# Routing scatters of a mixture-of-experts stage: order of the last group's powers, and how many scatters are under way

## What is computed

```python
probs = softmax(x @ Wr)                       # x: the normed tokens, N = 32*112
w_topk, e_topk = top_k(probs, 2)
e_flat = e_topk.reshape(-1)
pos = cumsum(one_hot(e_flat)) - 1, taken at e_flat
keep = pos < 1024
buf = zeros(8, 1024, 256).at[e_flat, pos].set(repeat(x, 2), mode='drop')
h = rms(buf, norm_w)
buf_out = (gelu(h @ Wg) * (h @ Wu)) @ Wd + buf
contrib = w_topk * buf_out[e_flat, pos] * keep
out = x + contrib.sum   # tokens that overflowed take a small shared expert instead
```

## Time and profile before

| | |
|---|---|
| median of 3 runs | 3072.48 us |
| lowest and highest | 3069.31 and 3073.73 us |
| span of the profiled execution | 3069.1 us, the only time shown of it |
| busy: PE, DVE, ACT, POOL | 2945.7, 2030.9, 1448.5, 650.4 us |
| DMA | 185.47 MB, mean 60 GB/s |

### The profile page before, as it was taken

One profiled execution on the slowest core, in us unless ns is written; L12 is line 12 of the kernel. 1 busy time (PEld: TensorE's weight loads), 2 busy tenths in 40 slices (PEclk: granted clock), 3 DMA queues, 4 the chain that ended last, 5 costly groups with the idle time before them and its releaser, 6 DMA issues. The chain is left out here.

```text
span 3069.1 us, 61161 instructions
## 1 busy us (share of the span) xinstructions
PE 2945.7 (96%) x23332; PEld 2275.7 (74%) x23332; DVE 2030.9 (66%) x4378; ACT 1448.5 (47%) x2845; POOL 650.4 (21%) x952
## 2 busy tenths in 40 slices
PE   8997999989899999999999999799999999899999
PEld 6874656567799999999999999577777777556444
DVE  5773111138577887788888877566767666589664
ACT  3431111126455555555555555476666666556000
POOL 4565000046100220013012200212212112036000
PEclk9997999999899999999999999899999999899999
DMA  9643233249300000000000000000000000337100
GB/s 292 214 128 106 82 117 110 88 144 299 104 1 2 1 2 1 2 1 1 2 1 2 1 2 1 24 25 22 17 22 22 17 22 17 106 108 227 51 14 21
DMA packets 79537, 185.47 MB, mean 60 GB/s; under 512 B 12981, under 2 KB 23202, under 8 KB 78916
## 3 DMA queue, kind: packets, MB, share of 16 engines
q1 hardware_dynamic: 62708, 141.50, 14.3%
q10 hardware_dynamic: 10208, 25.30, 2.8%
q0 software_dynamic: 6336, 14.76, 1.7%
HBM read 150.26 MB, written 27.79 MB: 58 GB/s over the span
## 5 line engine op out<-in xcount | busy, mean ns | idle before, releaser
L2792 DVE CUSTOM_DVE_ANT_0 probs<-ps,add 112x375 f32<-112x375 f32 x512 | 258.9, 544 | 82.7 <-PE ps L2945 76.0
L2871 ACT ACTIVATE probs<-probs,neg_top 112x375 f32<-112x375 f32 x512 | 278.5, 600 | 63.5 <-DVE neg_top L2792 60.1
L1734 DVE TENSOR_TENSOR hidden<-gated,ps 128x512 f32<-128x512 f32 x64 | 44.0, 687 | 294.7 <-PE ps L1777 294.7
L2972 PEld LDWEIGHTS ps<-ident,probs 112*125 112x125 f32 x1536 | 196.8, 188 | 44.4 <-issue 16.7
L2351 DVE TENSOR_REDUCE top<-ps 112x16 f32<-112x1792 f32 x96 | 194.2, 2023 | 46.1 <-PE ps L2590 45.9
L2972 PE MATMUL ps<-ident,probs 112*125 112x112 f32 x1536 | 219.7, 279 | 1.8 <-DVE probs_t L2799 1.8
L3416 PE MATMUL ps<-we,xn_t 128*128 128x512 f32 x448 | 201.9, 614 | 1.7 <-PEq L846 0.9
L2367 DVE TENSOR_TENSOR probs<-probs,inv_sum 112x1792 f32<-112x1792 f32 x96 | 196.0, 2042 | 3.3
L2355 DVE TENSOR_TENSOR probs<-ps,top 112x1792 f32<-112x1792 f32 x96 | 194.3, 2024 | 3.3
L2363 DVE TENSOR_REDUCE row_sum<-probs 112x16 f32<-112x1792 f32 x96 | 193.9, 2020 | 3.2 <-ACT probs L2475 3.2
L2558 PE MATMUL ps<-ident,probs 112*112 112x112 f32 x1536 | 179.8, 260 | 8.2 <-ACT probs_t L2470 7.3
(11 more groups left out here) (464 smaller groups left out, 6276.8 us busy)
## 6 DMA issues: line engine op xcount, KB each, us to landing
ctx_t<-in_ctx_T_dram SPq DMA_DIRECT2D x96, 375.0 KB, 4.5
ctx_sb<-in_ctx_dram ACTq DMA_DIRECT2D x64, 384.0 KB, 4.5
ctx_sb<-in_ctx_dram SPq DMA_DIRECT2D x32, 384.0 KB, 8.9
ctx_sb<-in_ctx_T_dram SPq DMA_DIRECT2D x32, 375.0 KB, 3.1
queue<-zeros SPq DMA_DIRECT2D x32, 256.0 KB, 5.1
rows<-queue SPq DMA_DIRECT2D x16, 512.0 KB, 4.9
outputs<-out SPq DMA_DIRECT2D x16, 512.0 KB, 2.9
mask_in<-in_mask_BxSxS_fk_dram SPq DMA_DIRECT2D x16, 328.1 KB
```

The lines of the kernel that those rows point to most:

```text
L2792: dve.tensor_tensor_reduce(out=probs[:, u, h, :], in0=k.ps[0:S, SCORE + h, 0:L], in1=add[:, j % 2, :], scale=1.0, scalar=BIG, op0=ALU.add, ...
L2871: act.activation(probs[:, u, h, :], probs[:, u, h, :], ACT.Exp, bias=neg_top[:, u, h:h + 1], scale=-1.0).then_inc(s["probs_done"], 1)
L2972: mm = pe.transpose(k.ps[0:KR, PT + h % 2, r * S:(r + 1) * S], probs[:, n % 3, h, r * KR:(r + 1) * KR], k.ident[0:S, 0:S])
```

## The change

Only POOL's instruction list changes. In `shared_scatters`, `token_sizes` and `token_inverses` of group 3 stand ahead of the 32 scatters. The stop behind every fourth scatter is gone; instead each scatter adds to one of three semaphores in turn (`landed[0..2]`), and before scatter i POOL waits until scatter i - 3 has landed. At the end it waits for all three. Groups 0 and 1 keep their own semaphores and waits. `token_scatter` takes the semaphore as an argument.

```diff
-    t.scattered = [sem(nc, f"scattered{g}") for g in range(B // G)]
+    t.scattered = [sem(nc, f"scattered{g}") for g in range(LAST - 1)]
+    t.landed = [sem(nc, f"landed{i}") for i in range(UNDER_WAY)]
...
+UNDER_WAY = 3
...
 def shared_scatters(k, w, t, pool):
 
     token_half_scales(k, w, pool, GH * (LAST + 1) - 1)
-    for g in (LAST - 1, LAST):
-        for n in range(G * TOP_K):
-            token_scatter(k, t, pool, g, n)
-            if g == LAST - 1 and n == 3:
-                token_sizes(k, w, pool, LAST)
-            elif g == LAST - 1 and n == 7:
-                token_inverses(k, w, pool, LAST)
-            if n % 4 == 3:
-                pool.wait_ge(t.scattered[g], 16 * (n + 1))
-    for g in range(LAST + 1):
+    token_sizes(k, w, pool, LAST)
+    token_inverses(k, w, pool, LAST)
+    count = 2 * G * TOP_K
+    for i in range(count):
+        g, n = divmod(i, G * TOP_K)
+        if i >= UNDER_WAY:
+            pool.wait_ge(t.landed[i % UNDER_WAY], 16 * (i // UNDER_WAY))
+        token_scatter(k, t, pool, LAST - 1 + g, n, t.landed[i % UNDER_WAY])
+    for i in range(UNDER_WAY):
+        pool.wait_ge(t.landed[i], 16 * len(range(i, count, UNDER_WAY)))
+    for g in range(LAST - 1):
         pool.wait_ge(t.scattered[g], 16 * G * TOP_K)
```

More of the change, by code:

```diff
@@ L321, in scatter @@
                         for n in (2 * turn, 2 * turn + 1):
-                            token_scatter(k, t, pool, g, n)
+                            token_scatter(k, t, pool, g, n, t.scattered[g])
                 opening_constants(k, w, o, s, pool)
@@ L1395, in token_rows, with token_scatter @@
     dve.tensor_copy(t.put_at[:, g, :, :], t.put_f).then_inc(t.s["put_ready"], 1)
-def token_scatter(k, t, pool, g, n):
+def token_scatter(k, t, pool, g, n, landed):
     j, r = divmod(n, TOP_K)
@@ L1403, in token_scatter @@
     pool.indirect_dma_start(k.queue[:, :], bass.IndirectOffsetOnAxis(ap=t.put_at[:, g, r, j:j + 1], axis=0), t.xr[g][:, j, :], None,
-                            bounds_check=ROWS - 1, oob_is_err=False).then_inc(t.scattered[g], 16)
+                            bounds_check=ROWS - 1, oob_is_err=False).then_inc(landed, 16)
 def token_gains(k, w, t, dve, g):
```

## The result

The changed kernel took 3075.94 us (median of 20 runs, 3068.61 to 3083.76) beside 3072.60 of the kernel before on the same chip: a ratio of 1.0018, 95% interval 1.0010 to 1.0026. In a later series it stood at 1.0001 (0.9988 to 1.0013). So it is as fast as before or up to 0.3% slower, and certainly not 0.46% faster. The forecast of 3058.3 was wrong. The profiled execution took 3073.92 us, its span is 3072.1.

A forecast was written before the change was run, and what follows sets the result against it. POOL's last scatter start bounds the block's end, POOL ending 8.7 us behind DVE. Powers 0.84 us later and stops 15.0 us less give -14.15 us: 3058.3 us against the median of 3072.48; range 3054 to 3063 (8 in 10).

The forecast's parts named there:

- Part 1: Group 3's powers move ahead of the scatters on POOL: first scatter starts 0.84 us later, 225.40 instead of 224.56.
- Part 2: POOL's 31 scatter steps without stops take 38.7 us instead of 53.69, 1.25 each, waits free: 15.0 us less.
- late landings: Rival at the wait ahead of each scatter: landings come late in an unbroken row; +9.6 us, 3082 us; 3%.
- a broken overlap: Rival on POOL: a wait stops early preparation of the next scatter; step 1.64, -2.8 us, 3069.6 us; 7%.
- Part 3: DVE has group 3's row numbers ready at 243.8, 0.9 us before the 17th scatter needs them.
- the slack of 0.9: Margin in us between group 3's row numbers being ready on DVE (243.8) and being needed (244.7).
- Part 4: At the block's end DVE ends at 269.5, POOL's drain at 272.0: POOL last by 2.5, all 14.15 us arrive.
- the signs of being wrong: Profile signs: gaps over 0.4 us before scatters, the 17th waiting on DVE, DVE's or PE's drain behind POOL's, later expert-stage wait.
- The rule weighed: Two-input DVE instructions and GpSimd SBUF reads lock each other out; the gain would be 7.6 us instead of 14.15.
- The early powers help nobody: Rival: DVE's chain is held by something else, row numbers come at 251.8 as before; -7.0, 3065.5 us; 4%.
- the 9.56 us: DVE's wait for `r_inv` in the kernel before, until 238.85; with early powers `r_inv` was forecast at 224.9.
- row numbers late: Rival: PE's third gate and up run at half speed; group 3 starts at 247.6, not 245.4; -11.9, 3060.5 us; 8%.

The follow-up runs named there:

- the second trace: Repeat of the changed kernel with rows of four and a 112 x 4 power after each fourth scatter; ratio to the kernel before 0.9976 (0.9966 to 0.9987).

## Why the prediction was wrong

- **Part 1, the powers: right.** The first scatter starts 222.46 - 216.65 = 5.81 us behind the start of the last half power, against 225.40 - 219.66 = 5.74 forecast.
- **Part 2, the stops: right for POOL by itself.** Steps of 1.25, the waits between scatters free, a landing about 2.6 us after its scatter's start also in an unbroken row. Fifteen steps behind the 17th scatter take 19.4 us, 18.8 were forecast. The rivals of late landings and of a broken overlap are out. (The forecast's 245.4 for the 17th scatter is 245.5 by its own steps; nothing hangs on it.)
- **Part 3 is the step that failed.** It let DVE run its chain from the logits at the durations that it had beside rows of four: ready for the 17th scatter 24.1 us into the tail (243.8 - 219.66). It was 38.0 (254.67 - 216.65). The start on the logits is 5.2 us of the 13.9, the stutter of the searches 4.1, the CAST 4.8; what follows took 0.2 less than forecast. Less the slack of 0.9, and with 0.2 more from the row numbers to the scatter, they are the 13.1 us by which the 17th scatter was late (38.9 for 25.7). The chain itself was costed well: with rows of four and powers early, the row numbers were ready at 22.4 us (238.34 - 215.95), for 24.1 forecast, and DVE's drain began at 47.3, for 48.9 (269.5 - 0.9 - 219.66).
- **Part 4 failed for the same reason.** DVE's work behind the row numbers met the third group's unbroken row, with gelus 2.6 and 4.2 us late, DVE's multiplication at 278.49 5.9 late, and DVE ended 4.5 us behind POOL instead of 2.5 ahead. Together: POOL's last scatter stood at 58.2 us instead of 44.4 (264.1 - 219.66), and DVE added 4.5 at the barrier; these 18.3 us are what lies between the tail that was forecast, 53.45, and 71.73. Both had been named among the signs of being wrong, the 17th's wait on DVE and a drain behind POOL's. The drain of POOL is indeed constant: 5.29 us in every trace.
- **The rule weighed** (the Trainium skill, SBUF — State Buffer, section "SBUF: two separate sides") did not take back what it would have: descriptions beside DVE's runs took 0.94 to 1.3 us. The other engines' lateness is not of its kind either, since ACT has it too.
- **The rivals.** "The early powers help nobody" comes nearest, but the row numbers were not as late as before, they were 5.9 us later (38.0 us into the tail for 32.1), and the mechanism is another: the chain was not held by something that the 9.56 us hid, it was held by the new row. The condition of "row numbers late" came true in the changed kernel: the third gate and up products took 3.35 us each behind idle stretches, the up product at a granted clock of 0.50, the lower level of 1.2 GHz (247.0 to 250.4). But the gate product lay inside DVE's lateness and cost nothing, which about makes up for the 1.7 us that the up product took longer; both are inside the "0.2 less". With rows of four the two took 1.67 and 1.77, as the forecast had it. No rival had the new row delay another engine.
- **Range and chances.** I gave 0.90 to faster because no doubt was about what POOL's row does to another engine: two were about POOL's own path, two about a chain on DVE and PE that I took from the trace with shorter rows. The evidence for the failure stood in the same list of waits as the row that I started from.

## What to carry to other kernels

A change that packs one engine's indirect transfers closer is costed on that engine and also on those that run beside it; look in the old trace for the closest row that there is, and at what the others did just then, above all at waits whose releaser the view can't name. When an engine that issues scatters is the last at a barrier, its stops may have been protecting others: shorten them step by step rather than take them away. Here rows of four scatters with one small instruction between them gave 0.25%, the unbroken row gave nothing.

## What the runs showed of the hardware

- Indirect scatters of 112 rows issued by POOL every 1.25 us hold up the start of instructions on ACT and DVE. In the tails of the changed kernel single starts were 2.0 to 7.0 us late, and gaps of 0.6 to 1.9 us stood between searches of DVE that wait for nothing; PE and POOL kept their pace. The first late instruction was due behind the fourth scatter of the first row (227.30) and beside the twelfth of the second (269.45). This stays when the rows carry no data (33.3 us of "remote" waits), and when there are no waits between scatters (34.8 us).
- A pause nearly ends it: with a step of 2.2 us after every fourth DVE was 0.7 us late at the logits (1.1 in the second trace) and nobody was at other places, with 1.75 it was not enough (2.5 us at the logits, 25.3 us of "remote" waits). POOL may be busy with other work in the pause.
- POOL's drain took 5.29 us in all 17 traces of this block's end.
- **Open:** which resource it is, and whether what comes late is the semaphores or the instructions themselves; the gaps between searches show that it isn't semaphores alone. POOL's making of the descriptions and the DMA engines' work on their packets were not told apart; no run changed the number of rows in a scatter.
